# Dense feed-forward layer, attention over the best keys and router logits: three stages merged into one unrolled pipeline, and a search that counts in PSUM

## The reference, cut to what matters

```
x = x + L0_xattn(layernorm(x), ctx)
x = x + L0_ffn(layernorm(x))       # residual + (abel * (1-gate) + nonabel * gate)
    abel    = gelu(xn @ aw1 + ab1) @ aw2 + ab2             # 512 hidden
    nonabel = rotate(sum over the best 2 of 6 experts: w_e * (gelu(xn @ ew1[e]) @ ew2[e]))
    gate    = sigmoid([abel, nonabel] @ gc_w + gc_b)
x = x + L1_xattn(layernorm(x), ctx, top_k=32)
    scores  = (q @ k.T) / sqrt(128)                        # 64 keys for each row
    softmax over the 32 highest scores of the row, times v, times Wo, plus bo
x = x + L1_ffn(layernorm(x))       # router: logits = xn @ Wg, 16 experts, 320 rows each
```

## Time and profile before

| | us |
|---|---|
| median of 3 runs (lowest, highest) | 1389.11 (1388.62, 1389.3) |
| the profiled execution | 1394.12 |
| its span, first to last instruction | 1392.2 |
| busy in the span: TensorE, VectorE, ScalarE, GpSimd | 1074.5, 879.3, 576.3, 457.4 |
| mean granted clock of TensorE, of full speed | 0.821 |

### The profile page before, as it was taken

One profiled execution on the slowest core, in us unless ns is written; L12 is line 12 of the kernel. 1 busy time (PEld: TensorE's weight loads), 2 busy tenths in 40 slices (PEclk: granted clock), 3 DMA queues, 4 the chain that ended last, 5 costly groups with the idle time before them and its releaser, 6 DMA issues. The chain is left out here.

```text
span 1392.2 us, 21924 instructions
## 1 busy us (share of the span) xinstructions
PE 1074.5 (77%) x6382; PEld 793.4 (57%) x6382; DVE 879.3 (63%) x2955; ACT 576.3 (41%) x1180; POOL 457.4 (33%) x592
## 2 busy tenths in 40 slices
PE   3788879999995677566496378867999999568842
PEld 1656659989994455432464256545567667445621
DVE  7667755665664676599622777766344436547768
ACT  2466434444442444332032256521334345446521
POOL 1444201000010244361363834302770457324311
PEclk9799969999998555555588569966999999869975
DMA  8333010000000600314042444200347752044202
GB/s 269 93 110 109 25 31 1 1 1 1 0 1 0 182 20 19 98 24 121 21 108 64 109 112 107 53 1 25 89 142 195 219 156 52 20 121 125 73 3 61
DMA packets 112674, 103.16 MB, mean 74 GB/s; under 512 B 11120, under 2 KB 92400, under 8 KB 112176
## 3 DMA queue, kind: packets, MB, share of 16 engines
q1 hardware_dynamic: 80816, 76.32, 19.3%
q0 software_dynamic: 6400, 12.92, 3.5%
q10 hardware_dynamic: 25344, 12.59, 3.1%
HBM read 64.23 MB, written 37.75 MB: 73 GB/s over the span
## 5 line engine op out<-in xcount | busy, mean ns | idle before, releaser
L858 DVE TENSOR_REDUCE mha_nm<-mha_pS 128x16 f32<-128x1024 f32 x96 | 117.1, 1220 | 24.6 <-PE mha_pS L620 24.4
L798 POOL TENSOR_TENSOR mha_ks<-KS,w_ctx 104x1024 fp32r<-104x1024 f32 (+1 forms) x48 | 90.8, 1894 | 96.2 <-POOLq L100 51.7
L1529 ACT ACTIVATE ffn_hid<-ffn_pH,w_ffn 128x512 f32<-128x512 f32 x128 | 85.6, 688 | 55.3 <-PE ffn_pH L1452 54.6
L741 ACT ACTIVATE XH<-mha_pST 128x1024 f32<-128x1024 f32 x96 | 97.8, 1019 | 11.3 <-PE mha_pST L641 11.2
L620 PE MATMUL mha_pS<-mha_ks,mha_qs 96*128 96x256 f32 (+1 forms) x384 | 80.5, 337 | 24.9 <-DVE mha_nm L858 19.8
L1465 PEld LDWEIGHTS ffn_pE<-W2R,ffn_hid 128*128 128x128 f32 x768 | 94.6, 194 | 4.4 <-issue 0.2
L1641 DVE SCALAR_TENSOR_TENSOR ffn_acc<-ffn_pE,ffn_wt,ffn_acc 128x128 f32<-128x128 f32 x192 | 54.0, 343 | 66.9 <-PE ffn_pE L1465 66.9
L1465 PE MATMUL ffn_pE<-W2R,ffn_hid 128*128 128x128 f32 x768 | 95.2, 278 | 0.0
L620 PEld LDWEIGHTS mha_pS<-mha_ks,mha_qs 96*128 96x128 f32 (+1 forms) x384 | 59.1, 213 | 41.1 <-issue 21.4
L2546 POOL DMA_INDIRECT leaf_rows<-XH,tree_place x64 | 63.1, 985 | 55.3 <-DVE tree_place L2626 36.1
L1557 POOL TENSOR_TENSOR X<-X,ffn_xh 128x512 f32<-128x512 f32 (+1 forms) x8 | 10.3, 1283 | 211.1 <-DVE ffn_xh L1587 211.1
(11 more groups left out here) (527 smaller groups left out, 2890.4 us busy)
## 6 DMA issues: line engine op xcount, KB each, us to landing
mha_qs<-queries SPq DMA_DIRECT2D x72, 256.0 KB, 4.0
tree_leaf<-in_leaves_dram SPq DMA_DIRECT2D x96, 96.5 KB
queries<-mha_qh SPq DMA_DIRECT2D x24, 256.0 KB, 2.1
queries<-mha_ql SPq DMA_DIRECT2D x24, 256.0 KB, 2.5
leaf_rows<-top_none SPq DMA_DIRECT2D x12, 512.0 KB, 6.6
tree_xs<-leaf_rows ACTq DMA_DIRECT2D x24, 256.0 KB, 3.5
leaf_results<-tree_ys ACTq DMA_DIRECT2D x24, 256.0 KB, 3.9
EW<-in_L_W_dram SPq DMA_DIRECT2D x32, 128.0 KB, 2.5
```

Of the source, the lines that this page charges most:

```text
L741: act.activation(PT[b % PB][:, CU * i:CU * i + CU, :], pST[:], ACT.Exp, scale=SC).then_inc(s["P"], 1)
L798: pool.tensor_tensor(ks[b % KB][0:K1, :, :, :], kb, hb, ALU.mult).then_inc(s["k"], 1)
L858: dve.tensor_reduce(nm[:, t, :], pS[:], AX.X, ALU.max, negate=True).then_inc(s["nm"], 1)
L1529: act.activation(hid[p % 2][:, c, :], pH[c][:], ACT.Gelu, bias=b).then_inc(s["h"], 1)
```

## The change

The feed-forward stage, the preparing stage and the stage of attention over the best keys become one stage, `ffn_and_top`, with the names ffn_.... Its loop is written out, with no hardware loop: 8 slots for the 8 groups and 4 more, each of eight passes. The attention over the best keys works on groups of four tiles as well and runs one to four slots behind: in slot n the queries' input of group n-1, the queries, scores and search of group n-2, the results of group n-3, and the rows and router logits of group n-4. What of this stands behind which pass is written in `extras` for TensorE and ScalarE and in the loops of VectorE and GpSimd. Keys and values are made in slots 0 and 1, and the masks in slot 1. `final` moves from behind combine 5 to behind combine 2. To fit PSUM's eight banks, pX takes the place of pX, pG and pI, and pQ and pY each serve several steps of the attention in turn; most of its buffers are single instead of double. The router's logits are copied by ScalarE to SBUF (LG, in the space of XH), and the back-load of rows into XH waits until they are read. The clears of the leaf rows are issued at the head of the merged stage. In the routing stage the count reads the values in PSUM, and the copy goes.

The diff, cut to its core:

```diff
-def attention_top(core):
...
-def ffn_moe_rotated(core):
...
+def ffn_and_top(core, masks):
...
+        pX, pA, pQ, pY = (st.ps(n, [P, 512]) for n in ("pX", "pA", "pQ", "pY"))
+        pH = [st.ps(f"pH{u}", [P, 512]) for u in range(2)]
+        pE = [st.ps(f"pE{u}", [P, GT, P]) for u in range(2)]
...
+            for k in range(NG):
+                sp.wait_ge(s["x2"], k + 1)
+                sp.dma_start(core.xd[GT * P * k:GT * P * k + GT * P, :].rearrange("(t p) d -> p t d", p=P), x2[:]).then_inc(core.rows_out, 16)
...
+            def q_turn(k):
+                need(pe, s["xq"], k + 1)
+                need(pe, s["sc"], k)
+                for j in range(GT):
+                    ins = pe.transpose(pQ[:, P * j:P * j + P], xq[:, j, :], ident)
+                ins.then_inc(s["xqp"], 1)
...
+            def kept_turn(k):
+                need(pe, s["pk"], k + 1)
+                need(pe, s["lgo"], k)
+                for j in range(GT):
+                    ins = pe.transpose(pY[:, P * j:P * j + P], pk[:, j, :], ident)
+                ins.then_inc(s["PTp"], 1)
...
+            def extras(n, p):
+                if n == 0 and p in (2, 4):
+                    keys_values(p // 2 - 1)
+                if (n, p) in ((0, 6), (1, 0)):
+                    values_out(2 * n)
+                    values_out(2 * n + 1)
+                if (n, p) == (1, 4):
+                    pe.wait_ge(s["we"], 4)
+                    for on_tensor, _, _ in mask_prep:
+                        on_tensor(pe)
+                if p == 0 and ffn(n - 2):
+                    queries(n - 2)
+                if p == 1 and ffn(n - 2):
+                    scores(n - 2)
+                if p == 1 and ffn(n - 4):
+                    rows_turn(n - 4)
+                if p == 2 and ffn(n - 4):
+                    route_logits(n - 4)
+                if p == 3 and ffn(n - 3):
+                    kept_turn(n - 3)
+                if p == 4 and ffn(n - 3):
+                    results(n - 3)
+                if p == 7 and ffn(n - 1):
+                    q_turn(n - 1)
...
+            for n in range(SLOTS):
                 for p in range(NP):
+                    if ffn(n):
+                        up(n, p)
+                    if n == 0 and p == 1:
+                        weights_T(0)
+                        bias_rows(0)
+                    if p > 0 and ffn(n):
+                        down(n, p - 1)
+                    if p == 0 and ffn(n - 1):
+                        down(n - 1, NP - 1)
+                        if ffn(n):
+                            bias_rows(n)
+                    if ffn(n + 1) and ffn(n):
                         if p == 3:
+                            x_transposes(n + 1)
                         if p == 4:
+                            logits(n + 1)
                         if p == 7:
+                            weights_T(n + 1)
+                    extras(n, p)
...
+            def exponentials(k):
+                need(act, s["nm"], k + 1)
+                need(act, s["pk"], k)
+                for j in range(GT):
+                    ins = act.activation(ex[:, j, :], sc[:, j, :], ACT.Exp, bias=nm[:, j:j + 1])
+                ins.then_inc(s["P"], 1)
...
+            def extras(n, p):
+                if n == 0 and p in (2, 4):
+                    keys_values(p // 2 - 1)
+                if (n, p) in ((0, 6), (1, 0)):
+                    values_out(2 * n)
+                    values_out(2 * n + 1)
+                if p == 0 and ffn(n - 2):
+                    queries(n - 2)
+                if p == 0 and ffn(n - 4):
+                    rows(n - 4)
+                if p == 1 and ffn(n - 4):
+                    rows_turned(n - 4)
+                if p == 2 and ffn(n - 4):
+                    route_logits(n - 4)
+                if p == 3 and ffn(n - 3):
+                    kept_turned(n - 3)
+                if p == 6 and ffn(n - 1):
+                    for_queries(n - 1)
+                if p == 7 and ffn(n - 1):
+                    q_turned(n - 1)
+                if p == 7 and ffn(n - 2):
+                    exponentials(n - 2)
...
+            residual(0)
+            for n in range(SLOTS):
+                if ffn(n - 1):
+                    add_abel(n - 1)
+                if ffn(n + 1):
+                    residual(n + 1)
+                if ffn(n - 1):
+                    query_scales(n - 1)
+                if ffn(n - 3):
+                    row_scales(n - 3)
+                if ffn(n - 1):
+                    bias(n - 1)
...
+            def best8(k, r):
+                if r == 0:
+                    dve.wait_ge(s["sc"], k + 1)
+                src = sc if r == 0 else wk
+                for j in range(GT):
+                    ins = dve.max(m8[:, j, r, :], src[:, j, :])
+                best(ins)
+                if r == 0:
+                    dve.tensor_scalar(nm[:], m8[:, :, 0, 0], -1.0, None, ALU.mult).then_inc(s["nm"], 1)
+                for j in range(GT):
+                    ins = dve.match_replace(wk[:, j, :], m8[:, j, r, :], src[:, j, :], MARK)
+                best(ins)
...
+            for n in range(SLOTS):
+                if ffn(n - 1):
+                    tail(n - 1)
+                for p in range(NE):
+                    if ffn(n):
+                        combine(n, p)
+                    if p == 0 and ffn(n - 1):
+                        tail_gate(n - 1)
+                    if p == 1 and ffn(n) and ffn(n + 1):
+                        normalise(n + 1)
+                    if p == 2 and ffn(n - 1):
+                        final(n - 1)
+                    if p == 3 and ffn(n) and ffn(n + 1):
+                        split(n + 1)
+                    if p >= 3 and ffn(n) and ffn(n + 1):
+                        gating(n + 1, p - 3)
+                    if p == 4 and ffn(n - 3):
+                        add_results(n - 3)
+                    if p == 4 and ffn(n - 2):
+                        scaled(n - 2)
+                        best8(n - 2, 0)
+                    if p == 5 and ffn(n - 2):
+                        for r in range(1, TOP // R8):
+                            best8(n - 2, r)
+                        keep(n - 2)
+                    if n == 1 and p == 2:
+                        dve.wait_ge(core.mask3_loaded, 16)
+                        for _, first, _ in mask_prep:
+                            first(dve)
+                    if n == 1 and p == 5:
+                        for _, _, second in mask_prep:
+                            second(dve)
...
-        pL = core.pL
+        LG = core.LG
...
-            link(dve.tensor_copy(MT, pM[:]))
...
-                dve.scalar_tensor_tensor(hit, MT, at, ones, op, ALU.mult, accum_out=cnt[:, 0:1]).then_inc(s["cnt"], 1)
+                dve.scalar_tensor_tensor(hit, pM[:], at, ones, op, ALU.mult, accum_out=cnt[:, 0:1]).then_inc(s["cnt"], 1)
...
+            sp.wait_ge(s["dx"], 1)
...
+        core.LG = core.XH[:, 0:T * N1 // P, :].rearrange("p t d -> p (t d)")
...
-            ffn_moe_rotated(core)
...
-                prep_top(core, masks)
-                core.pL = kept.enter_context(nc.psum_tensor("logits", [P, T * N1], F32))
-                attention_top(core)
...
+                ffn_and_top(core, masks)```

The order of VectorE's instructions in a slot of the middle. First before, from the end of gating's second part, behind combine 4, to the statistics of the group before:

```order
L1618 TENSOR_REDUCE ffn_sm<-ffn_pr 128x4
L1619 TENSOR_TENSOR ffn_ob<-ffn_pr,ffn_sm 128x24
L1623 TENSOR_TENSOR ffn_sm<-ffn_sm 128x4
L1641 SCALAR_TENSOR_TENSOR ffn_acc<-ffn_pE,ffn_wt,ffn_acc 128x128 x4
L1626 TENSOR_SCALAR ffn_sm<-ffn_sm 128x4
L1627 TENSOR_SCALAR ffn_sm<-ffn_sm 128x4
L1628 TENSOR_TENSOR ffn_oa<-ffn_oa,ffn_sm 128x24
L1629 TENSOR_TENSOR ffn_ob<-ffn_ob,ffn_sm 128x24
L1630 TENSOR_TENSOR ffn_wt<-ffn_oa,ffn_ob 128x24
L1667 TENSOR_SCALAR ffn_gz<-ffn_gz 128x4
L1673 SCALAR_TENSOR_TENSOR X<-ffn_acc,ffn_gz,X 128x128 x4
L1677 BN_STATS ffn_bn<-X 128x6 x4
```

More of the change, by code:

```diff
@@ new lines, in kept_turned, with rows @@
+            def kept_turned(k):
+                need(act, s["PTp"], k + 1)
+                need(act, s["Y"], k)
+                act.activation(PT[:], pY[:], ACT.Copy).then_inc(s["PT"], 1)
+            def rows(k):
+                need(act, s["r2"], k + 1)
+                need(act, s["x2Tp"], k)
+                need(act, core.rows_out, 16 * k)
+                for j in range(GT):
+                    ins = act.activation(x2[:, j, :], X[:, GT * k + j, :], ACT.Identity, bias=nb2[:, j:j + 1], scale=rs2[:, j:j + 1])
+                ins.then_inc(s["x2"], 1)
@@ L1714, in _ @@
             for part in range(3):
[L1715 to L1719 removed]
+                gating(0, part)
+            for n in range(SLOTS):
+                if ffn(n - 1):
+                    tail(n - 1)
+                for p in range(NE):
+                    if ffn(n):
+                        combine(n, p)
[3 more added lines that the diff above has]
```

(4 more changed lines are left out.)

768 lines of the change are left out of this document (271 added, 497 removed).

## The result

The changed kernel takes 1343.3 us (median of four runs, 1339.4 to 1346.3) and the kernel before, run beside it, 1389.0 us: a ratio of 0.967, 95% interval 0.9644 to 0.9695. Forecast were 1331 us and 1311 to 1350. So sign, mechanism and range held, and 12 of the 58 us forecast did not come; A's own range, 1321 to 1339, is missed by 4 us. The medians leave out slow executions, of which there was one, of 3204.6 us (experiment 3, 11 products); what slowed it no run shows.

A forecast was written before the change was run, and what follows sets the result against it. TensorE bounds the feed-forward stage; the preparing and best-keys attention stages (146 us) are no engine's. Merging saves 51.5 us and the count 6.4, together 58, so 1389.1 us becomes 1331, range 1311 to 1350.

The forecast's parts named there:

- A: Merged stage: VectorE's pass 4 work is late for the weights, full slots 36.5 us; 1331 us, range 1321 to 1339, chance 0.52.
- TensorE's own work in a slot, 33.3 us: Full slots 4 to 6: 28.9 us of feed-forward plus 4.4 us of added attention work, if TensorE waits for nothing.
- The place and length of the wait: At the transpose of the gate's weights: VectorE needs 9.4 us after expert 4, so TensorE stands 3 us.
- Rival B: Merged stage: TensorE never waits as VectorE runs further ahead; full slots 33.3 us, 15 us more saved, 1316 us, chance 0.19.
- the granted clock 1.00 from slot 1 to 7: Expected sign in the merged stage: TensorE's granted clock stays at 1.00 in slots 1 to 7.
- rival D: Merged stage: standing 3 us in 36 drops TensorE's clock to 0.50, 30 us more per slot; chance 0.04 for two or more.
- Slot 1: VectorE sets this slot: start after 9.7 us, then 16, final part 3.0 and masks 4.5, in all 33.2 us.
- Drain, 90 us: Slot 7 and the uncovered chain after it, to the merged stage's end at 530 us: 90 us.
- kept scores to their result, 4.5 us: In the drain: from kept scores to their result 2.42 us for two tiles before, taken as 4.5 for four.
- Table loads and PSUM access: ScalarE's switch costs 1.30 us without a further drain; VectorE's count from PSUM takes 0.751 us, no slower than from SBUF.
- The count, 6.4 us: Routing stage: counts reading PSUM lose GpSimd's disturbance (5.7 us) and the copy (0.69 us), ending it 6.4 us earlier.
- C: Merged stage: GpSimd's big additions meet VectorE's two-SBUF-source instructions, 16 us in five slots; 1347 us, chance 0.20.

The follow-up runs named there:

- experiment 3: Changed kernel with 11, and twice with 13, unused 128x512 products on TensorE before its wait for the gate's weights, slots 3 to 6: 1344.4, 1341.2 and 1341.7 us.
- experiment 2: Changed kernel with VectorE adding results and doing the whole search behind the gate's weights, only scaling left between combines 4 and 5: 1329.6 us, 0.9562 of the kernel before.
- experiments 2 and 8: 2: changed kernel, gate's weights ahead of search, 1329.6 us; 8: that plus results ahead of rows and logits in late slots, masks' first part in slot 0, 1308.2 us.
- experiment 7: Changed kernel with the copy to SBUF back and counts reading it: 1350.0 us; separately, kernel before with only the count reading PSUM, no copy: 1384.4 us.

## Why the prediction was right, and where it was off

- **TensorE's own work in a slot, 33.3 us**: nearly right, 33.67 (experiment 2).
- **The place and length of the wait**: right. VectorE's 9.4 us were 9.7, TensorE stood 3.16 to 3.18 us in slots 4 to 6, 0.67 in slot 2 and 3.08 in slot 3. Rival B, no wait, was a matter of VectorE's order only; experiment 2 made its slots true, at 1330 us instead of its 1316.
- **The slots, "the granted clock 1.00 from slot 1 to 7"**: this step failed. After the stalls before slots 4, 6 and 7 the clock fell to 0.50, for some 3, 6 and 3 us. I had rival D only as whole slots at 0.50, 30 us each; its short form, 1.6 us in slot 4 and 2.6 in slot 6 against slot 5, I did not price. Three slots took 115.2 us, forecast 109.5: 5.7 us, of them 4.3 the falls and the rest 0.5 us a slot (TensorE's work 0.37, the wait 0.15). The sum had a slip of its own: 36.3 + 0.3 is 36.6, not 36.5. Slots 2 and 3 took 31.9 and 35.7 us, forecast 31.3 and 35.3.
- **Slot 1**: 36.7 us, forecast 33.2. I had made it VectorE's; it was TensorE that stood 4.0 us for the masks and then ran some 3 us at half clock. Slot 0 was 3.4 us better than forecast (227.1 against 230.5), and that is luck: from 197.5 to 205 us the granted clock was 0.99 in this profile and 0.50 in that of before, from which the forecast was made. In the profiles of experiments 2 and 8, with 0.50 there, slot 0 ended at 230.0 and 230.3.
- **Drain, 90 us**: 92.8. VectorE's terms were exact (the final part at +46.7 of +46.8, group 6 searched at +57.8 of +58.0). The term "kept scores to their result, 4.5 us" was taken for the chain alone; the queue ahead of it on TensorE made it 8.0 and 5.4.
- **Table loads and PSUM access**: the terms from this case's rows held (1.30 us; 0.75 us).
- **The count, 6.4 us**: right, 5.9 (experiment 7).
- **The sum.** By stages 48.1 us came of 57.9. The medians show 45.7. The 3.4 us of slot 0 are in the 48.1, a difference of the two profiles and not of the kernels; the rest of the gap is within what single executions differ.

A came, with a clock term that moves it 5 us towards C; by time alone 1343 lies outside A's own range and near C's 1347, and it is the slots, with 1 us for the meetings instead of 3.2, that tell the two apart. What stays open: why the clock falls behind the stalls before slots 4, 6 and 7 and not behind the one before slot 5, equally long; and why the later stages are longer with products in the stalls.

## What to carry to other kernels

When engines of unequal load are merged in one pipeline, ask of each instruction on which the fullest engine waits what stands ahead of it in its producer's queue, and put everything that is not due there behind it: here that order alone was 14 us of 1343. Price a stall of the fullest engine above its length, since the clock may fall behind it, and try to take the stall away: filling it gained nothing in the whole time here. And write out the drain as queues, not as a chain: what is harmless beside other work in a full slot is on the path there.

## What the runs showed of the hardware

A stall of TensorE of 3.1 us was followed in three of four places by some 3 to 6 us at 0.50, in the same places in three profiles of the changed kernel (in one of four places with the masks moved); with 2.6 or 3.1 us of products in the stall it was not. Two kernels with a mean granted clock of 0.86 and 0.84 in the 80 us from the token took about as long from there to the end (709.7 and 709.1 us) as the changed kernel with 0.88 (708.6 in the same profile). Two operations of VectorE on 128x4 and 128x24 took 0.63 and 0.66 us instead of 0.17 and 0.18 beside GpSimd additions, all from SBUF: such a meeting costs small operations as well as the large ones of the earlier trace rows.
